# A recurrence and slice-attention stage: block-diagonal products as 64x64 quarters, moved behind the token sums, and a fill with more loads and paced gathers

## What is computed

```python
h = h + experts(layernorm(h))                     # y_tok = ybuf[idx, pos] * (prb * kept): a gathered row, scaled
# recurrence: the 16 images are the time steps, the 3137 tokens the batch
xp = einsum('tbi,hi->tbh', layernorm(h), W_ih) + b_ih + b_hh
h_new = tanh(xp_t + h_old @ W_hh.T)               # for t = 0..15
h = h + hiddens
# slice attention, 8 heads, 64 slices, on y = layernorm(h)
x_mid, fx_mid = y @ W_x + b_x, y @ W_fx + b_fx
weights = softmax((x_mid @ W_slice + b_slice) / temp)       # per token and head, over the slices
token = einsum('bhnc,bhng->bhgc', fx_mid, weights) / (weights.sum(tokens) + 1e-5)
q, k, v = token @ W_q, token @ W_k, token @ W_v
out = softmax(q @ k.T * D**-0.5) @ v
h = h + einsum('bhgc,bhng->bhnc', out, weights) @ W_out + b_out
```

## Time and profile before

| | |
|---|---|
| time, median of 3 runs | 3404.04 us (3399.71 to 3404.74) |
| time of the profiled execution | 3396.83 us |
| its span, first to last instruction | 3395.0 us |
| mean granted clock of PE | 0.958 |
| busy, share of the span: PE, DVE, ACT, POOL | 88%, 75%, 64%, 59% |
| stage E: fill, up to the first logits | 1940 to 2009.4 us |
| stage E: turns with logits | 2009.4 to 3326 us |
| stage E: turns behind the last logits | 3326 to 3395 us |

### The profile page before, as it was taken

One profiled execution on the slowest core, in us unless ns is written; L12 is line 12 of the kernel. 1 busy time (PEld: TensorE's weight loads), 2 busy tenths in 40 slices (PEclk: granted clock), 3 DMA queues, 4 the chain that ended last, 5 costly groups with the idle time before them and its releaser, 6 DMA issues. The chain is left out here.

```text
span 3395.0 us, 66757 instructions
## 1 busy us (share of the span) xinstructions
PE 2993.6 (88%) x24922; PEld 1674.3 (49%) x24922; DVE 2534.9 (75%) x3280; ACT 2167.5 (64%) x3082; POOL 2001.1 (59%) x1191
## 2 busy tenths in 40 slices
PE   8999999969988989885599768899999999999997
PEld 6777777735555555553244323344444444444444
DVE  7888888868888888882387537777777777777773
ACT  6666666658777777761244346676766667676762
POOL 7777777712788888886100156556565565656531
PEclk9999999989999999996799969999999999999999
DMA  1111111111122121111454411111212112121102
GB/s 45 40 37 38 39 40 40 37 56 45 50 67 65 56 59 52 52 46 40 137 152 151 133 34 32 34 51 41 57 46 53 48 50 53 46 52 49 48 26 53
DMA packets 208262, 191.09 MB, mean 56 GB/s; under 512 B 76381, under 2 KB 163398, under 8 KB 207562
## 3 DMA queue, kind: packets, MB, share of 16 engines
q1 hardware_dynamic: 173850, 142.95, 14.7%
q0 software_dynamic: 25600, 26.01, 3.4%
q10 hardware_dynamic: 8496, 17.87, 1.4%
HBM read 99.08 MB, written 87.65 MB: 55 GB/s over the span
## 5 line engine op out<-in xcount | busy, mean ns | idle before, releaser
L2363 POOL TENSOR_TENSOR E_w<-E_w,E_rs 128x1024 f32<-128x1024 f32 x200 | 409.1, 2046 | 496.9 <-DVE E_rs L2271 496.9
L2356 POOL DMA_INDIRECT E_row<-yb,P_gi x400 | 394.3, 986 | 399.9 <-POOLq L93 306.1
L647 POOL DMA_INDIRECT xb<-B_yt,P_gi x400 | 531.7, 1329 | 115.5 <-issue 114.7
L203 POOL TENSOR_TENSOR A_kmask<-A_ksb,A_pack_a 128x3584 f32<-128x3584 f32 x56 | 356.5, 6366 | 150.5 <-ACT A_ksb L350 150.5
L2256 DVE TENSOR_REDUCE E_mx<-E_lg 128x16 f32<-128x1024 f32 x200 | 242.2, 1211 | 191.6 <-PE E_lg L1919 191.6
L2155 ACT ACTIVATE E_w<-E_w 128x1024 f32<-128x1024 f32 x200 | 211.6, 1058 | 266.1 <-DVE E_w L2264 229.0
L2268 DVE TENSOR_REDUCE E_sm<-E_w 128x16 f32<-128x1024 f32 x200 | 243.9, 1219 | 126.5 <-ACT E_w L2155 119.7
L432 DVE COPY A_vbd<-A_v 128x512 f32<-128x512 f32 x392 | 248.8, 680 | 15.2 <-PE A_v L290 15.1
L1950 PEld LDWEIGHTS E_wt<-S_pack_f,E_w 128*128 128x128 f32 (+1 forms) x1600 | 170.3, 141 | 166.9 <-issue 146.1
L2264 DVE TENSOR_TENSOR E_w<-E_lg,E_mx 128x1024 f32<-128x1024 f32 x200 | 244.8, 1224 | 6.4
L2140 ACT ACTIVATE E_wts<-E_wt 128x512 f32<-128x512 f32 (+1 forms) x400 | 213.4, 586 | 50.9 <-PE E_wt L1950 49.8
(11 more groups left out here) (322 smaller groups left out, 6965.7 us busy)
## 6 DMA issues: line engine op xcount, KB each, us to landing
R_xs<-xb SPq DMA_DIRECT2D x57, 256.0 KB, 2.7
yb<-R_ys SPq DMA_DIRECT2D x57, 256.0 KB, 2.0
B_x<-h SPq DMA_DIRECT2D x25, 512.0 KB
h<-B_hh SPq DMA_DIRECT2D x25, 512.0 KB
A_xg<-in_xw SPq DMA_DIRECT2D x56, 224.0 KB, 3.0
h<-A_res ACTq DMA_DIRECT2D x56, 224.0 KB, 2.0
E_hx<-h SPq DMA_DIRECT2D x48, 256.0 KB
out<-E_ob SPq DMA_DIRECT2D x96, 128.0 KB
```

The lines of the kernel that those rows point to most:

```text
L203: nc.gpsimd.tensor_tensor(kmask[i % 2][:], bc(ksb[i % 2][:].unsqueeze(2), [128, J, H, Q]), bc(head_of_row[:].unsqueeze(1).unsqueeze(3), [1 ...
L647: pool.indirect_dma_start(out=xb, out_offset=bass.IndirectOffsetOnAxis(ap=routed.gi[0:k, c, b:b + 1], axis=0), in_=yt[c % LT][0:k, D * row ...
L2356: pool.indirect_dma_start(out=row[b % LR][:, k, i], out_offset=None, in_=yb, in_offset=bass.IndirectOffsetOnAxis(ap=idx[:, c, 2 * n + i:2 ...
L2363: TT(w3, w3, bc(rs[g % 3][:].unsqueeze(2), [128, 2 * SH, G]), ALU.mult).then_inc(w_done, 1)
```

## The change

Four things, all in stage E:

- center_in and inputs become one function, center_and_inputs(s), and variance and variance_out become variances(s). Each 128x128 product is written as two 64x64 quarters, and the quarters of the two products alternate: across(i) takes row half i of the weights and of the data into output half 1 - i of PI, along(i) into half i of PO. The two images swap halves in center's product and swap back in mean's. A function waits for all that its two products need before its first quarter.
- center_and_inputs stands behind the token sums of the turn instead of ahead of them, and first_hidden behind the transposes of the weights, with a new wait for ih_done. On ACT the two copies of step 2 (ut and vb) move ahead of square_in and first_tanh.
- SP loads x of four blocks (LX) at the start, and in the loop only from block 4 on.
- POOL, in the turns before the first logits, waits ahead of each tile's gathers until the block of that turn is weighed (sc_done).

```diff
--- before.py
+++ after.py
@@ -1830,14 +1830,14 @@
 
                 sp.dma_start(prob[:].rearrange("p c b -> p (c b)"), keepp).then_inc(tables, 16)
                 sp.dma_start(pack[:], a["pack_d"]).then_inc(consts, 16)
-                for b in range(2):
+                for b in range(LX):
                     load_x(b)
                 for u in range(-LEAD, TURNS + 1):
                     s, t, _ = slot(u + LEAD)
                     left, done = u - LAG, u - LAG - 1
                     if t == 0:
                         at_block(store_h, s - 2)
-                        if s:
+                        if s + 1 >= LX:
                             at_block(load_x, s + 1)
                     if u == LAG - 3:
                         for i in range(2):
@@ -1863,9 +1863,30 @@
                         last = turn(PI[:, TILE * k:TILE * k + TILE], row[b % LR][:, k].rearrange("p b d -> p (b d)"), ident)
                     last.then_inc(tr_done, 1)
 
-                def center_in(b):
-                    pe.wait_ge(x_done, b + 1)
-                    mm(PI[:, 0:wide(b)], center, x[b % LX][:, 0:wide(b)], start=True, stop=True).then_inc(cen_done, 1)
+                def across(i, to, weights, b, data, **kw):
+                    return mm(to[HALF[1 - i], 0:wide(b)], weights[HALF[i], HALF[i]], data[HALF[i], 0:wide(b)],
+                              start=True, skip_group_check=True, **kw)
+
+                def along(i, to, weights, b, data, **kw):
+                    return mm(to[HALF[i], 0:wide(b)], weights[HALF[i], HALF[i]], data[HALF[i], 0:wide(b)],
+                              start=True, skip_group_check=True, **kw)
+
+                def center_and_inputs(b):
+                    first, second = 0 <= b < BLOCKS, 0 <= b - 1 < BLOCKS
+                    if first:
+                        pe.wait_ge(x_done, b + 1)
+                    if second:
+                        pe.wait_ge(y_done, b)
+                        after(pe, hc_done, b - 1)
+                    for i in range(2):
+                        if first:
+                            cen = across(i, PI, center, b, x[b % LX], stop=True)
+                        if second:
+                            ih = along(i, PO, wih, b - 1, sr, stop=b - 1 < J)
+                    if first:
+                        cen.then_inc(cen_done, 1)
+                    if second:
+                        ih.then_inc(ih_done, 1)
 
                 def turn_y(b):
                     pe.wait_ge(yo_done, b + 1)
@@ -1877,20 +1898,29 @@
                         last = turn(PI[:, TILE * k:TILE * k + TILE], yo[b % LY][:, TILE * k:TILE * k + TILE], ident)
                     last.then_inc(ty_done, 1)
 
-                def variance(b):
-                    pe.wait_ge(sq_done, b + 1)
-                    after(pe, yk_done, b - 2)
-                    mm(PI[:, 0:wide(b)], mean, sr[:, 0:wide(b)], start=True, stop=True).then_inc(var_done, 1)
-
-                def inputs(b):
-                    pe.wait_ge(y_done, b + 1)
-                    after(pe, hc_done, b)
-                    mm(PO[:, 0:wide(b)], wih, sr[:, 0:wide(b)], start=True, stop=b < J,
-                       skip_group_check=True).then_inc(ih_done, 1)
+                def variances(b):
+                    first, second = 0 <= b < BLOCKS, 0 <= b - 2 < BLOCKS
+                    if first:
+                        pe.wait_ge(sq_done, b + 1)
+                        after(pe, yk_done, b - 2)
+                    if second:
+                        pe.wait_ge(sq2_done, b - 1)
+                        pe.wait_ge(hc_done, b - 1)
+                        pe.wait_ge(tb_done, min(b, BLOCKS))
+                    for i in range(2):
+                        if first:
+                            var = across(i, PI, mean, b, sr, stop=True)
+                        if second:
+                            var2 = along(i, PO, meany, b - 2, sy[b % 2], stop=True)
+                    if first:
+                        var.then_inc(var_done, 1)
+                    if second:
+                        var2.then_inc(var2_done, 1)
 
                 def first_hidden(b):
                     if b >= J:
                         pe.wait_ge(tb_done, b - J + 1)
+                        pe.wait_ge(ih_done, b + 1)
                         mm(PO[HALF[0], 0:wide(b)], whh[HALF[1], :], hid[HALF[1], cols(b)],
                            start=False, stop=True, skip_group_check=True).then_inc(ha_done, 1)
 
@@ -1903,12 +1933,6 @@
                     pe.wait_ge(h_done, b + 1)
                     after(pe, ln2_done, b)
                     mm(PO[:, 0:wide(b)], center, x[b % LX][:, 0:wide(b)], start=True, stop=True).then_inc(cen2_done, 1)
-
-                def variance_out(b):
-                    pe.wait_ge(sq2_done, b + 1)
-                    pe.wait_ge(hc_done, b + 1)
-                    pe.wait_ge(tb_done, min(b + 2, BLOCKS))
-                    mm(PO[:, 0:wide(b)], meany, sy[b % 2][:, 0:wide(b)], start=True, stop=True).then_inc(var2_done, 1)
 
                 def logits(g):
                     b, k, _ = slot(g)
@@ -2049,11 +2073,7 @@
                         product(k)
                     elif 0 <= k < TILES:
                         turn_back(k - 1)
-                    if t == 1:
-                        at_block(center_in, s)
-                        at_block(inputs, s - 1)
-                        at_block(first_hidden, s - 1)
-                    elif t == 2:
+                    if t == 2:
                         at_block(second_hidden, s - 1)
                         at_block(turn_y, s - 3)
                     if step == 1:
@@ -2066,14 +2086,17 @@
                         zsum(z)
                     if begins(k) and width(k) == 1:
                         turn_back(k)
+                    if t == 1:
+                        center_and_inputs(s)
                     if 0 <= z < TILES:
                         turn_w(z)
+                    if t == 1:
+                        at_block(first_hidden, s - 1)
                     if t == 0:
                         at_block(turn_rows, s)
                         at_block(center_out, s - 2)
                     if t == end:
-                        at_block(variance, s)
-                        at_block(variance_out, s - 2)
+                        variances(s)
 
             @block.scalar
             def _(act):
@@ -2183,6 +2206,11 @@
                         A(mo[:].rearrange("p b q d -> p (b q d)"), WT[:, BANK[1]], ACT.Copy).then_inc(moc_done, 1)
                     if 0 <= u < TILES:
                         exponential(u)
+                    if step == 2:
+                        act.wait_ge(ut_done, n + 1)
+                        A(ut[:].rearrange("p q g -> p (q g)"), WT[:, BANK[1]], ACT.Copy).then_inc(utc_done, 1)
+                        act.wait_ge(vb_done, n + 1)
+                        A(vb[:].rearrange("p q b d -> p (q b d)"), WT[:, BANK[0]], ACT.Copy).then_inc(vbc_done, 1)
                     if t == 0 and logs:
                         at_block(root_in, s - 1)
                         at_block(root_out, s - 3)
@@ -2193,12 +2221,7 @@
                     elif t == 2:
                         at_block(second_tanh, s - 1)
                         at_block(by_token, s - 3)
-                    if step == 2:
-                        act.wait_ge(ut_done, n + 1)
-                        A(ut[:].rearrange("p q g -> p (q g)"), WT[:, BANK[1]], ACT.Copy).then_inc(utc_done, 1)
-                        act.wait_ge(vb_done, n + 1)
-                        A(vb[:].rearrange("p q b d -> p (q b d)"), WT[:, BANK[0]], ACT.Copy).then_inc(vbc_done, 1)
-                    elif step == 3:
+                    if step == 3:
                         act.wait_ge(asub_done, n + 1)
                         A(at, at, ACT.Exp, scale=D ** -0.5).then_inc(aexp_done, 1)
                     if begins(k) and width(k) == 1:
@@ -2367,6 +2390,8 @@
                 for u in range(-LEAD, TILES + 1):
                     if 0 <= u - 1 < TILES:
                         normalise(u - 1)
+                    if u < 0:
+                        pool.wait_ge(sc_done, slot(u + LEAD)[0] + 1)
                     if u + LEAD + AHEAD < TILES:
                         fetch(u + LEAD + AHEAD)
 
```

## The result

The changed kernel takes **3326.26 us** (median of 4 runs, 3321.40 to 3330.48); the kernel before, in the same comparison, 3401.88 (3397.99 to 3404.74). The ratio is 0.9781, 95% interval 0.9769 to 0.9793: faster by 74 us, where 69 was forecast, and inside the range. The sum was near, its terms were not: the fill gave 9.5 us less than forecast, the eight pairs 16.6 more, so the nearness of the sum is in part luck.

What follows compares the result with a forecast made beforehand. PE was taken to bound the middle pairs, something else the fill. Savings of 53 (six middle pairs), 4 (first pair), 4 (last pair) and 8 (fill), 69 us, from the median 3404.0 gave 3335 us, range 3306 to 3376.

Steps and rivals of the forecast that it cites:

- the fill: Stretch ahead of the first logits: paced gathers stop POOL 7.5 us earlier; 8 us saved, bounds 0 and 18; loads 0.
- The price of a set: Four 64x64 quarters of 512 columns take 1.02 us, as in stage B, instead of 1.92 for two 128x128 products.
- Rivals 3 and 4: In the sets: row halves take turns at a bank (3396 to 3404, 0.09); quarters run one after another (3604, 0.05).
- Six middle pairs: Pairs of the last stage between first and last: 8.8 us saved in each, 53 us in all.
- the step on the move: Center and wih behind the token sums: costs 0, or at most some 0.5 us at each of 7 sites.
- the raw sum: PE time saved by quarters before losses: 5.40 us in turns t==1 plus 4.54 in last turns, 9.94 a pair.
- rival 1: Pairs and fill: everything comes through, no turn bound by DVE; 88 us saved, 3316, pair period 158.2; chance 0.15.
- The cover: Token sum ahead of center's wait for E_yo; if too short, up to 1 us lost at 7 sites a pair.
- rival 2: Pairs and fill: DVE's chain and merged waits take back half; 35 us saved, 3369; chance 0.18.
- What doesn't reach the end: In each pair, DVE's chain takes back 0.5 us at blocks' ends and 0.6 behind step 3, 1.1 in all.
- First and last pair: First pair: less than half the raw sum, 4 us; last pair: about 11 of 25 turns keep blocks, 4 us.
- The inference on the gather stream: In the fill, POOL's gathers hold up signals of PE's work; 18 us saved if the lateness goes wholly.

Runs made afterwards that it cites:

- move_only: Kernel before with only the reordering: 128x128 products behind the token sums, first_hidden behind the transposes, ACT's two copies ahead; ratio 0.9907 to the kernel before.
- q_only: Kernel before with only the quarters, in the old places ahead of the token sums, and the old fill; ratio 1.0012 to the kernel before.
- q_early: Quarters in the old places, old fill, ACT making E_yo ahead of its copies of the transposed weights at t = 1; ratio 0.9857 to the kernel before.
- quarters_moved: Changed kernel with the fill of before (two loads at the start, no pacing of gathers); ratio 0.9793 to the kernel before.
- no_pacing: Changed kernel without the pacing of the gathers, still with four loads at the start; ratio 0.9786 to the kernel before.
- gap: Changed kernel plus a short multiplication on POOL ahead of each tile's gathers in the fill; 3311 us, ratio 0.9737 to the kernel before.
- fill_only: Kernel before with only the four loads at the start and the paced gathers, 128x128 products in the old places; ratio 0.9986 to the kernel before.
- q_hold: Quarters in the old places, old fill, ACT making E_yo ahead of its weight copies only in the first pair; ratio 0.9968 to the kernel before.
- early_gap: Changed kernel plus E_yo made ahead of ACT's weight copies and a POOL multiplication between tiles' gathers in the fill; 3303.58 us, ratio 0.9721.

## Why the prediction was right, and where it was not

- **The price of a set: right.** 1.02 us was taken and 1.02 measured, both row halves into one bank included. Rivals 3 and 4 fall: from the second pair on, at the full clock, no set that is followed without a wait takes over 1.02 us. With 384 columns on both sides a set took 0.81 where 0.78 was scaled. The rule of the Trainium skill that was weighed ("TensorEngine Tiling (Array Packing)", Gotcha 1) would have made the set 1.9 to 2.0; this trace doesn't agree with it, for quarters that write different partition halves of the bank.
- **Six middle pairs, 53 against 61.9: mis-sized.** Most of the missing 9 us, 1.1 a pair, is the step on the move, which was costed at nothing: "nothing is paid twice", but there was something to gain. The turns t = 1 save 6.5 to 7.0 us a pair, where the raw sum had 5.40. The move is worth 2.8 us a pair alone (move_only): the output product and the token sum cost less next to each other, 0.15 us a turn in the changed kernel, where t = 1 saves 1.05 instead of 0.90, and 1.02 instead of 0.67 in the three-tile block where PE waits for E_yo. Another 2.4 us are the pair behind the first one, which went from 169.7 to 157.4. So the pair period, 158.2 in the mean of the other five, is the one that the prediction set as rival 1's sign, and not its own 159.4; but what rival 1 denied, losses on the way to the end, is there, and the move makes up for it. The Trainium skill, "TensorEngine Tiling (Array Packing)", Key Properties, says that a change of the tiling mode drains TensorE; that the product (128x64 tiles) takes 1.78 us ahead of a 128x64 product, and 1.87 ahead of others, agrees with it.
- **The cover, named and right.** The prediction said that the token sum stands ahead of the wait for E_yo, and what is lost if the cover is gone: up to 1 us at each of 7 sites. Without the move exactly that happens, and more where the clock falls: in q_only the turns t = 1 gain nothing, in most pairs they lose over 2 us, and q_early, which only makes E_yo earlier, gets most of the gain back. So rival 2's mechanism (merged waits) is real; here the order of the same change takes it away.
- **What doesn't reach the end.** Blocks' ends: 0.08 of 0.58 lost where 512 columns meet 384 (6.33 to 5.83), as forecast (0.1); DVE's maxima are 5.52 us apart where 5.6 was taken as the least. Token attention: 0.6 was taken behind step 3 as a longer wait of 0.92. It did become longer, by 0.32 (0.92 to 1.24), and the turn of step 4 with it; step 3's own turn gains 0.32 of 0.58, and the turn of step 1 is 0.46 longer (6.81 to 7.27). Some 1.0 us a pair in all, so the term had the right sign and little over half of the size.
- **First and last pair, 4 and 4 against 9.0 and 6.7.** I took less than half in the first pair because PE waits there for 27 us. In this profile nearly the whole raw sum came through (157.3 to 148.3); in those of quarters_moved, no_pacing and gap, with the same program in this pair behind another fill, it took 150.4, 149.6 and 152.0, so 5 to 9 us were saved. Why PE's waits there didn't take more was not tried.
- **The fill, 8 against -1.5: wrong.** One of the prediction's own signs of being wrong came up in the changed kernel's profile: the lateness lasts as long with the paced gathers as without, and the first logits come at 2010.9, not at 2001. On 128x128 products pacing is worth 7 us (fill_only), from the stop that was worked out (7.5). With quarters the size is the same by the means, but not from that stop, so there the agreement is in part luck. What failed in the sum is the term beside it, "with one merged product in the part that sets the end", taken as a gain: quarters lengthen the fill, by about 4.4 us between the means. And the changed kernel's profile is at the slow end of its own spread. Whether the 4.4 are the merged waits (center waits there for signals that are late) or the larger number of PE instructions was not tried apart.
- **Late signals: shown.** The inference on the gather stream holds (gap). The bound of 18 us for the whole removal was near: 18.3 from the mean of the fills with quarters and no pacing (73.0) to gap's 54.7, 15.5 from the changed kernel's own (70.2).

## What to carry to other kernels

Two block-diagonal products written as quarters, so that all four quarters of the array run at once, took hardly more than one of them (1.02 us against 0.97), but merging them merges their waits: the set starts when the latest input is there, so put something independent ahead of it, or make that input earlier, before counting the gain. Measure the parts of such a change alone: here the quarters were worth nothing in the time without the move. Where an engine's results seem to arrive late, look for a stream of indirect gathers without a pause; short pauses in it took the late waits away here, where holding some of the gathers back did not.

## What was not expected of the hardware

- While POOL issued indirect DMAs back to back (one each 1.25 us), consumers of PE's results went on up to 14 us after PE's work had ended (no_pacing, q_hold), from the 21st to 28th gather on; with some 0.65 us more for every two gathers (gap, early_gap), none was late by more than 0.8 us. What holds the signals back is not settled.
- Behind a wait of 1.87 us on PE the granted clock of the next 8 us was 0.57, after 1.00 in the ten before, and a turn of 7 us became one of 10.0 (q_only). Behind the same wait in the last two pairs it stayed at 1.00; what decides between the two is open.
